# One transfer for gate and up weights, and list entries taken four at a time, in a Mamba and mixture-of-experts kernel

## What is computed

```python
# Mamba: 256 inner channels, 16 states, one recurrence a channel and state over 2048 steps
h = dA_t * h + dBu_t                  # for each of the 16 states
y = sum over states of h * C_t
x = x + (y + xc * D) * silu(z) @ out_w.T
x = x + silu(gate) * val @ ffp_w.T    # the feed-forward
# mixture of experts over the normalised x: D = 128, F = 344, E = 8, K = 2
logits = xt @ Ws + bs
topk_w, topk_idx = top_k(logits, 2); topk_w = softmax(topk_w)
g = xt @ Wg[e];  u = xt @ Wu[e];  h = silu(g) * u;  y = h @ Wd[e]
out = sum over the two chosen e of topk_w * y
```

## Time and profile before

| | us |
|---|---|
| median of 3 runs | 938.18 |
| lowest, highest | 937.45, 941.28 |
| the profiled execution | 938.88 |
| its span, first to last instruction on the engines | 937.0 |
| granted TensorE clock, mean over the span | 0.799 |

### The profile page before, as it was taken

The page is one execution under the profiler, slowest core; times in us unless marked ns, Lnnn a source line. Parts: engine busy times, 40 slices in busy tenths (PEclk is TensorE's granted clock), DMA queues, the critical chain, the costliest instruction groups (busy, mean ns, idle before and its releaser), DMA issues.

```text
span 937.0 us, 13285 instructions
## 1 busy us (share of the span) xinstructions
PE 625.2 (67%) x3482; PEld 480.3 (51%) x3482; DVE 759.7 (81%) x1114; ACT 448.9 (48%) x924; POOL 592.9 (63%) x531
## 2 busy tenths in 40 slices
PE   4357387477857666876686768776886775554782
PEld 1144253365346345753574367635775663544782
DVE  1279899999899999999999999899999963241442
ACT  3446455644744474547454745474445532211331
POOL 1095376458557985898589858895688735263331
PEclk9578578658657878998798769976999997786997
DMA  7334233323323355434543454327665520474654
GB/s 179 110 119 130 85 127 93 112 93 126 114 83 99 112 156 162 153 96 139 167 143 95 142 169 137 105 81 234 176 178 157 164 60 20 118 201 129 201 172 126
DMA packets 98941, 123.31 MB, mean 132 GB/s; under 512 B 13047, under 2 KB 63043, under 8 KB 98851
## 3 DMA queue, kind: packets, MB, share of 16 engines
q1 hardware_dynamic: 94323, 113.07, 41.1%
q0 software_dynamic: 4544, 9.38, 2.8%
HBM read 110.42 MB, written 13.52 MB: 132 GB/s over the span
## 4 chain that ended last, share of the span: by engine, by line
DVE 40%; PE 23%; issue 20%; SPq 6%; ACT 5%; POOL 2%; DMA 2%; DVEq 1%; another core or an unknown queue 1%; POOLq 0%; ACTq 0%
DVE state L867 21%; DVE product L875 5%; PE work_front L1020 4%; PE y L1062 3%; PE work_front L1026 3%; PE gate L1139 3%; PE up L1146 3%; PE up L1156 2%; DVE stats L800 2%; DVE silu_m L985 2%; DMA y_back<-y_dram 1%; PE work_side L1082 1%; SPq L513 1%; SPq L523 1%; DVE conv L841 1%
## 5 line engine op out<-in xcount | busy, mean ns | idle before, releaser
L574 POOL TENSOR_TENSOR inflow<-du,b_wide 128x1024 f32<-128x1024 f32 x128 | 307.9, 2408 | 188.8 <-DVE product L875 149.1
L734 ACT ACTIVATE decay<-delta,a_neg 128x512 f32<-128x512 f32 x256 | 174.0, 689 | 188.2 <-DVE state L867 174.8
L1062 PE MATMUL y<-ident,product 128*128 128x128 f32 x1024 | 171.9, 323 | 108.9 <-DVE product L875 108.8
L867 DVE TENSOR_TENSOR_SCAN state<-decay,carry,inflow 128x512 f32<-128x512 f32 x192 | 235.1, 1265 | 1.0 <-ACT decay L734 1.0
L1062 PEld LDWEIGHTS y<-ident,product 128*128 128x128 f32 x1024 | 145.5, 170 | 159.7 <-DVE product L875 126.4
L875 DVE TENSOR_TENSOR product<-state,c_wide 128x1024 f32<-128x1024 f32 x128 | 192.9, 1507 | 2.8 <-PE y L1062 1.7
L656 POOL DMA_INDIRECT y_dram<-y_rows,x_rows x78 | 93.7, 1201 | 85.7 <-ACT y_rows L790 77.3
L595 POOL DMA_INDIRECT row_dram<-m_tok,place x64 | 72.4, 1131 | 22.0 <-issue 13.3
L867 DVE TENSOR_TENSOR_SCAN state<-decay,inflow 128x512 f32<-128x512 f32 x64 | 74.5, 1204 | 8.7 <-ACT decay L734 6.2
L1020 PE MATMUL work_front<-u_t,w_tap 128*128 128x512 f32 x128 | 65.7, 640 | 3.8 <-ACT u_t L684 1.7
L1156 PE MATMUL up<-w_down,h_cols 128*128 x336 | 53.3, 298 | 12.8 <-DVE h_cols L990 10.9
(11 more groups left out here) (175 smaller groups left out, 1083.1 us busy)
## 6 DMA issues: line engine op xcount, KB each, us to landing
b_wide<-bc_dram SPq DMA_DIRECT2D x128, 256.0 KB
c_wide<-bc_dram SPq DMA_DIRECT2D x128, 256.0 KB
w_stage<-in_Wg SPq DMA_DIRECT2D x78, 172.0 KB
w_stage<-in_Wu SPq DMA_DIRECT2D x78, 172.0 KB
x_rows<-row_dram SPq DMA_DIRECT2D x78, 65.0 KB
y_back<-y_dram SPq DMA_DIRECT2D x16, 256.0 KB
x_tok<-in_x SPq DMA_DIRECT2D x8, 256.0 KB, 6.1
out<-x_tok SPq DMA_DIRECT2D x8, 256.0 KB
```

What stands on the lines that cost most here:

```text
L574: e.tensor_tensor(inflow[:, key % 3], du[:, c % 2], b_wide[:, key % ROW_SLOTS:key % ROW_SLOTS + 1, :].to_broadcast([P, HALVES, CHUNK]), AL ...
L734: e.activation(decay_bank[h][:], delta[:, c % 2, h, :], ACT.Exp, scale=a_neg[:, h, n:n + 1]).then_inc(S["decay"], 1)
L867: e.tensor_tensor_scan(state[:, key % STATE_SLOTS, h, :], decay_bank[h][:], inflow[:, key % 3, h, :], 0.0 if c % (SEQ // CHUNK) == 0 else ...
L1062: t = e.matmul(y_bank[s // 2][:, y_at(s, h)], product[:, key % 2, h, s * P:(s + 1) * P], ident[:], is_transpose=True, start=False, stop=n ...
```

## The change

Two things are changed.

1. A tensor in DRAM, `gate_up_dram`, holds for each expert and each of the 128 rows the 344 gate weights and behind them the 344 up weights. Two transfers of 1.41 MB each (8 x 128 x 344 x 4 bytes), from DRAM to DRAM, fill it at the start, behind the last load of x. `load_w` then issues one transfer of 344 KB in place of two of 172 KB, and PE waits for 16 instead of 32 on its semaphore. The first `load_w` waits for the two copies.
2. `picks` takes up to four entries of a list into four registers by one load, at tiles with j = 0, 4, 8 and so on. It stands in `load_w`, in `load_x` and in PE's `down`. In place of 78 loads in each of the three there are 22. The check of each value against its limits stays: there are as many as before, but the four of a load now stand together.

```diff
+PICKS = 4
...
+        gate_up_dram = nc.dram_tensor("gate_up_dram", (EXPERTS, D_MODEL, 2, FF), f32, kind="Internal").ap()
...
+        def picks(engine, table, k, j, most):
+
+            return nc.values_load_multi_w_load_instructions(table[0:1, k, j:min(j + PICKS, TILES[k])], engines=(engine,), min_val=0, max_val=most)[1]
...
             for c in range(2, CHUNKS):
                 e.dma_start(x_tok[:, c], x_dram[c]).then_inc(S[f"d_x{c}"], 16)
+            for j, weights in enumerate(("Wg", "Wu")):
+                e.dma_start(gate_up_dram[:, :, j], T[weights]).then_inc(S["d_gate_up"], 16)
...
-                    expert = e.value_load(expert_i[0:1, k, j:j + 1], min_val=0, max_val=EXPERTS - 1)
+                    if j % PICKS == 0:
+                        experts = picks(mybir.EngineType.SP, expert_i, k, j, EXPERTS - 1)
+                    if key == 0:
+                        e.wait_ge(S["d_gate_up"], 32)
                     if key >= W_SLOTS:
                         e.wait_ge(S["up"], key - W_SLOTS + 1)
-                    e.dma_start(w_stage[:, q, 0, 0:FF], T["Wg"][bass.ds(expert, 1)].rearrange("o d f -> d (o f)")).then_inc(S[f"d_w{q}"], 16)
-                    e.dma_start(w_stage[:, q, 1, 0:FF], T["Wu"][bass.ds(expert, 1)].rearrange("o d f -> d (o f)")).then_inc(S[f"d_w{q}"], 16)
+                    e.dma_start(w_stage[:, q, :, 0:FF], gate_up_dram[bass.ds(experts[j % PICKS], 1)].rearrange("o d j f -> d (o j) f")).then_inc(S[f"d_w{q}"], 16)
...
-                    at = e.value_load(tile_i[0:1, k, j:j + 1], min_val=0, max_val=ROW_TILES - 1)
+                    if j % PICKS == 0:
+                        tiles = picks(mybir.EngineType.SP, tile_i, k, j, ROW_TILES - 1)
...
-                    e.wait_ge(S[f"d_w{key % W_SLOTS}"], 32 * (key // W_SLOTS + 1))
+                    e.wait_ge(S[f"d_w{key % W_SLOTS}"], 16 * (key // W_SLOTS + 1))
...
-                    expert = e.value_load(expert_i[0:1, k, j:j + 1], min_val=0, max_val=EXPERTS - 1)
+                    if j % PICKS == 0:
+                        experts = picks(mybir.EngineType.PE, expert_i, k, j, EXPERTS - 1)
```

More of the change, by code:

```diff
@@ L416, in mamba_moe_block @@
             + [f"d_rows{q}" for q in range(X_SLOTS)] + [f"d_w{q}" for q in range(W_SLOTS)] + [f"d_scatter{c}" for c in range(CHUNKS)]
-            + ["d_pads", "bases", "tag0", "tag1", "list", "listed_count", "merged"] + [f"d_y{q}" for q in range(Y_SLOTS)] + [f"d_merge{q}" for q in range(MERGE_SLOTS)]
+            + ["d_gate_up", "d_pads", "bases", "tag0", "tag1", "list", "listed_count", "merged"] + [f"d_y{q}" for q in range(Y_SLOTS)] + [f"d_merge{q}" for q in range(MERGE_SLOTS)]
             + ["halved", "a_exp", "a_neg", "diag", "minus_half", "ones", "ser_shift", "w_tap", "back_halved", "halo"]
@@ L522, in _ @@
                             e.wait_ge(S["d_pads"], 16 * (EXPERTS * (SPAN_OF[k] + 1) + 1))
-                    at = e.value_load(tile_i[0:1, k, j:j + 1], min_val=0, max_val=ROW_TILES - 1)
+                    if j % PICKS == 0:
+                        tiles = picks(mybir.EngineType.SP, tile_i, k, j, ROW_TILES - 1)
                     if key >= X_SLOTS:
                         e.wait_ge(S[f"d_y{key % Y_SLOTS}"], 16 * ((key - X_SLOTS) // Y_SLOTS + 1))
-                    e.dma_start(x_rows[:, q, :], row_tiles[bass.ds(at, 1)].rearrange("o p d -> p (o d)")).then_inc(S[f"d_rows{q}"], 16)
+                    e.dma_start(x_rows[:, q, :], row_tiles[bass.ds(tiles[j % PICKS], 1)].rearrange("o p d -> p (o d)")).then_inc(S[f"d_rows{q}"], 16)
             e.wait_ge(S["d_out"], 16 * CHUNKS)
@@ L1156, in _ @@
                         t = e.matmul(up[:, FF_WIDE:], h_cols[:n, key % 2, q, :],
-                                     w_down[:n, bass.ds(expert, 1), q, :].rearrange("p o d -> p (o d)"), start=q == 0, stop=q == NF - 1)
+                                     w_down[:n, bass.ds(experts[j % PICKS], 1), q, :].rearrange("p o d -> p (o d)"), start=q == 0, stop=q == NF - 1)
                     t.then_inc(S["down"], 1)
```

## The result

The changed kernel took 943.86 us (median of 20 executions, 936.88 to 953.81), the kernel before 938.41 beside it (934.28 to 942.25, 20). The ratio is 1.0041, 95% interval 1.0022 to 1.0060: 3.9 us slower, where 8 us less was forecast. (The medians of all 20 are 5.4 us apart.) So the profile read here is that of a second set, whose ratio is 1.0064 (1.0030 to 1.0098): span 945.5 us, clock 0.773, against 937.0 and 0.799 of the kernel before.

What follows compares the result with a forecast made beforehand. DVE was taken to bound the units and SP's queue round 7, with PE taking over there. Terms -0.5 - 0.2 - 0.5 + 0.8 - 2.8 - 5.0 = -8.2 us from 938.88 gave 930.7, so 930.0 at the median; range 926 to 936.5.

Steps and rivals of the forecast that it cites:

- I take nothing for it: In the units, DVE sets the pace and SP's fetches of B wait for POOL; SP's saving there counts 0 us.
- The load of four: On SP and PE, a load of four values costs between 0.30 and 1.20 us; 0.30 taken.
- Rival B: A load of four costs four loads, 1.20 us: about 938 us, or 934 at half that price; chance 0.10.
- The burst in the tail: On PE in round 7, three more checks before every fourth down product add 0.81 us; about 2.33 us a tile.
- The merge, -2.8: In round 7, y_back is issued 3 us earlier, so PE's 2.81 us wait for DVE goes: -2.8 us.
- the rest of round 7, -5.0: From 870.34 us to the last gate product, 17 tiles take 39.6 us on PE instead of 44.5: -5.0 us.
- Round 6, -0.5 and -0.2: SP from list's end to second row load takes 4.56 us instead of 5.04, -0.5; tiles 53 to 55 give -0.2.
- The copy, nothing: At the start, the 2.82 MB copy ends at 38.2 to 39.0 us, hidden before the first inflow at 44.54: 0 us.
- rival A: The copy gets half the engines or half the rate, 20 to 21 us; kernel 938 to 939 us; chance 0.07.
- Rival D: The copy takes over 20 us and delays the first inflow; 946 us at 100 GB/s; chance 0.04.
- C: Rival: something else, landings above all, holds the tail at 2.5 us a tile; 933 to 934 us; chance 0.12.
- E: Rival: PE's sequencer hides the checks, so charges of 0.8 and 3.2 us vanish; 926 us; chance 0.05.

Runs made afterwards that it cites:

- rows of 24: Both list tables padded from 22 to 24 columns, against the changed kernel: 1.0007 of the kernel before; with PE's single loads as well, 0.9929.

## Why the prediction was wrong, step by step

**The units, "I take nothing for it": the step that failed.** I asked there what SP saves, found it ending in waits, and closed the stage with "PE and POOL do not bound that stage either". But the change adds to PE too, and I costed PE's burst in the tail alone. In the units 12 groups stand ahead of gate products that ACT and DVE need in their order. The burst moved the down product from 1.07 to 2.13 us behind the transposes in the mean, and the units grew by 12.4 us. PE was not the engine with the most work, and it had no slack at these places. The same burst alone, in the kernel before, cost 8.2 us, and four single loads and checks in one piece 13. The forecast had named the sign, that it would be wrong as a whole if the units changed by more than 1 us, without a price or a chance for it; and profiles of the same work were up to 9.6 us apart there, so one profile could not have read that sign at 1 us.

**The load of four: 0.30 us, measured 0.33 or 1.0.** "Since the words stand side by side" holds where they begin at a multiple of 16 bytes from the table's start, and not 8 bytes past one. Rival B had four loads' price at 1.20 and was right on the duration in rounds 1, 3 and 7; it came to 938, since it too left the units at nothing. The Trainium skill, "DMA: Bandwidth & Descriptors", section "Latency and other measured facts", puts a floor of about 600 ns under `tensor_load`. The trace disagrees: 0.30 us for one value and 0.33 for four aligned ones are below it; four others take 1.0.

**The burst in the tail: 0.81 us each, measured 1.3 to 1.5 of idle PE.** Three checks were to stand open, "PE at 2.1 us for three tiles and 2.9 for the fourth". That path was right: PE did take over as the bound, at 2.12 us for most tiles and 3.70 to 3.86 for each of five with a burst. The size was off, by the unaligned load. The changed kernel's PE at the first burst of round 7:

```profile
875.09 0.83 PE L1158 MATMUL decay<-x_cols,w_stage 128*128 128x128 f32 x6
877.27 0.93 PE L1169 MATMUL y<-w_down,h_cols 128*128 x6 [1.34 <-issue]
```

With aligned loads the idle time is 0.7 to 0.8 us, as charged, and the fourth tile takes 3.03 to 3.15. Yet round 7 as a whole is only 1.0 us longer with the aligned bursts than without them (58.0 and 57.0, on two chips), where 0.8 + 3.2 were charged, since without them PE waited elsewhere.

**The merge, -2.8, and the rest of round 7, -5.0.** With aligned loads `y_back` came where it was forecast (11.42 us against 11.4), partly by luck: my sum counts four lists of 1.38 us, but only three stand behind the first transfer of the round, and each of the five weight transfers took 0.2 to 0.3 us more than charged. At SP's 0.87 us a load it was issued 13.11 us after the first transfer, so that three loads took 1.7 of the 2.8 us back. The whole stretch, 57.6 forecast, was met by 58.0 with bursts, but errors cancel in it: without them the same sum gives 57.6 - 4.0 = 53.6, and 57.0 was measured. There most of PE's tiles took 2.12 to 2.5 us, but one took 4.08, 1.7 of them waiting for its rows. SP had waited 4.6 us in all, in three places, for results of earlier tiles to land before it could load rows, a wait that the changed kernel has too (4.1 us), that the kernel before does not have in its round 7, and that the forecast has nowhere; that it made those rows late is likely, not tested.

**The merged transfer's issue, 0 to 0.15 more: measured 0.22** (0.56 us against 0.34). A tile on SP would then be 1.76 + 0.22 = 1.98 us, still under PE's.

**Round 6, -0.5 and -0.2: not found.** From the list's end to the second row load SP took 4.96 us, where 5.04 became 4.56 in the forecast; the two merged transfers at 0.22 more each are the 0.4 missing. The stretch up to round 7 was 1.1 us shorter in the changed kernel and, with rows of 24 and single loads on PE, 4.7 us longer than with the copies alone; but three profiles of unchanged work have 89.6, 85.5 and 90.1 us there, so a gain of 0.7 us can't be seen.

**The copy, nothing: right.** Windows at the start, columns as above:

```profile
24.00:36.00 12.00, 9.05 (x12) 2.62 (x12) 0.66 (x1) 3.81 (x5) 0.00 (x0) 0.56 1.02 317
```

All 16 engines are busy, at 317 GB/s with the x loads among it; half of them, rival A, would show half that share. By the rule quoted in the prediction from the Trainium skill, "DMA: Bandwidth & Descriptors", section "Why a DMA increments its semaphore by 16 and not by 1", 1024 rows use 16 engines; this window agrees. Rival D had a slower kernel, 946 us, and the time came near it, but by another path: D needed a late first fetch of B, and the first inflow was on time.

**C and E.** PE's waits from 876 to 925 us of the changed kernel:

```profile
PE up L1169 <- issue: 2.8, 2, 1.5
PE y L1169 <- issue: 2.8, 2, 1.4
PE decay L1169 <- issue: 1.3, 1, 1.3
PE y L1143 <- DMA x_rows<-row_dram: 0.5, 1, 0.5
```

Its own sequencer holds it for 6.9 us, always ahead of a down product, landings for 0.5. So C fell in this kernel, and E too: the sequencer hides one load and check, not four.

## What to carry to other kernels

Sequencer work that is free in small pieces is not free in one: the same loads and checks, gathered ahead of every fourth down product, cost 13 us here without one instruction more. Before batching register loads, find the place on each engine that takes them, in every stage, and ask who waits for the product behind; an engine that is idle a third of the time may have no slack there. Batch only what can be loaded from an aligned address, spread or drop the checks, and leave the merge of transfers, which paid by itself, apart from it.

## What the hardware showed that I had not expected

A register load of four words on PE took 0.33 us from a multiple of 16 bytes (counted from the table's start) and 1.0 to 1.2 us from 8 bytes past one; on SP 0.30 and 0.87. One word took 0.27 to 0.30 us, two words 0.47 to 0.54. And behind 1.8 to 2.6 us without a product the down product ran at the level of 1.2 GHz in 8 of 11 places; with products in their place it was 2, and in two profiles of the kernel before 0 and 1.
